# A Perceiver block on one core: self-attention's output projection as three float32r products

## The reference

```
x = x + xattn(layernorm(x), ctx, ctx)      # 16 heads of 16, Wq Wk Wv Wo with biases
x = x + attn(layernorm(x))                 # 16 heads of 16, causal, w_qkv, w_out with biases
x = x + ffn(layernorm(x))                  # ternary weights, rows scaled to 127 levels, SiLU gate, inner 1024

def attn(x):
    q, k, v = split(x @ w_qkv + b_qkv)     # heads of 16
    att = softmax(causal(q k^T / 4))
    return (att v) @ w_out + b_out         # the product that the change is about
```

## Time and profile before

| what | value |
|---|---|
| median of 3 runs | 918.96 us (917.99 to 919.00) |
| profiled execution, its own time | 916.78 us |
| span in it, first to last instruction | 915.0 us |
| PE busy | 876.1 us, 96% of the span |
| DVE busy | 758.4 us, 83% |
| ACT busy | 695.8 us, 76% |
| POOL busy | 431.2 us, 47% |
| mean granted TensorE clock | 0.997 |
| cross-attention, self-attention, feed-forward | about 0 to 550, 550 to 775, 775 to 915 us |

### The profile page before, as it was taken

The page is one execution under the profiler, slowest core; times in us unless marked ns, Lnnn a source line. Parts: engine busy times, 40 slices in busy tenths (PEclk is TensorE's granted clock), DMA queues, the critical chain, the costliest instruction groups (busy, mean ns, idle before and its releaser), DMA issues.

```text
span 915.0 us, 28319 instructions
## 1 busy us (share of the span) xinstructions
PE 876.1 (96%) x9666; PEld 732.9 (80%) x9666; DVE 758.4 (83%) x1587; ACT 695.8 (76%) x2046; POOL 431.2 (47%) x643
## 2 busy tenths in 40 slices
PE   6999999999999999999999988999999998899997
PEld 5888988888888888888988976887878775566664
DVE  5878878888888888877887777988888887999996
ACT  4787887776777777778777765777777767899996
POOL 3333334233333333333443226666666662777775
PEclk9999999999999999999999999999999999999999
DMA  6222111110111011111111100000000000001001
GB/s 181 96 90 80 41 46 29 42 49 30 40 46 40 29 46 40 36 39 40 46 29 40 34 2 1 3 1 1 1 0 0 1 2 2 24 30 35 29 32 39
DMA packets 31637, 31.86 MB, mean 35 GB/s; under 512 B 3280, under 2 KB 30800, under 8 KB 31568
## 3 DMA queue, kind: packets, MB, share of 16 engines
q1 hardware_dynamic: 30448, 30.47, 10.9%
q10 hardware_dynamic: 1120, 0.59, 0.2%
HBM read 26.86 MB, written 4.19 MB: 34 GB/s over the span
## 4 chain that ended last, share of the span: by engine, by line
PE 76%; ACT 12%; issue 5%; DVE 4%; POOL 2%; DMA 0%; ACTq 0%; POOLq 0%; SPq 0%; DVEq 0%
PE psum L342 11%; PE psum L297 9%; PE psum L329 9%; PE psum L312 9%; PE psum L368 6%; PE psum L665 4%; ACT probs L1017 4%; PE psum L703 3%; PE psum L377 3%; PE psum L714 3%; PE psum L284 3%; ACT probs L503 3%; PE psum L750 2%; PE psum L684 2%; PE psum L350 2%
## 5 line engine op out<-in xcount | busy, mean ns | idle before, releaser
L503 ACT ACTIVATE probs<-psum,nmax 128x256 f32<-128x256 f32 x512 | 237.3, 488 | 63.1 <-DVE nmax L460 62.3
L460 DVE TENSOR_REDUCE nmax<-psum 128x2 f32<-128x512 f32 x256 | 158.9, 682 | 24.3 <-PE psum L329 23.6
L511 POOL TENSOR_TENSOR rstd<-vare,minus_half 128x1 f32<-128x1 f32 x96 | 53.1, 553 | 153.8 <-DVE vare L398 151.3
L342 PE MATMUL psum<-id_sb,probs 128*128 128x128 f32 x1024 | 124.6, 273 | 0.5 <-ACT probs L503 0.5
L527 POOL TENSOR_TENSOR cl<-c_sb,ch 128x512 fp32r<-128x512 f32 x64 | 81.6, 1275 | 78.8 <-ACT ch L478 78.8
L342 PEld LDWEIGHTS psum<-id_sb,probs 128*128 128x128 f32 x1024 | 113.0, 140 | 3.4 <-ACT probs L503 2.8
L484 ACT ACTIVATE probsT<-psum 128x512 f32<-128x512 f32 x160 | 89.3, 603 | 30.7 <-PE psum L342 30.5
L503 ACT ACTIVATION_READ_ACCUMULATOR probs<-psum,nmax 128x1 f32 x512 | 112.6, 220 | 0.0
L534 POOL TENSOR_TENSOR rm<-rinv,hm_sb 128x256 f32<-128x256 f32 x64 | 39.7, 620 | 120.6 <-DVE rinv L437 120.6
L329 PE MATMUL psum<-k_sb,qb 32*128 32x256 f32 x1024 | 88.8, 400 | 3.8 <-DVE k_sb L413 1.8
L329 PEld LDWEIGHTS psum<-k_sb,qb 32*128 32x128 f32 x1024 | 62.2, 184 | 15.3 <-issue 10.8
(11 more groups left out here) (141 smaller groups left out, 2338.9 us busy)
## 6 DMA issues: line engine op xcount, KB each, us to landing
c_sb<-in_ctx_t SPq DMA_DIRECT2D x64, 256.0 KB, 2.7
x_sb<-in_x SPq DMA_DIRECT2D x32, 128.0 KB, 2.4
out<-y_sb SPq DMA_DIRECT2D x32, 128.0 KB, 1.7
w_all<-in_w_gate SPq DMA_DIRECT2D x1, 1024.0 KB, 6.4
w_all<-in_w_up SPq DMA_DIRECT2D x1, 1024.0 KB, 5.1
w_all<-in_w_down SPq DMA_DIRECT2D x1, 1024.0 KB, 6.6
wqkv_sb<-in_w_qkv SPq DMA_DIRECT2D x1, 768.0 KB, 5.7
wk_sb<-in_wk ACTq DMA_DIRECT2D x1, 256.0 KB, 3.8
```

What stands on the lines that cost most here:

```text
L342: last = nc.tensor.transpose(sp[g][:, c:c + P], probs[:, 2 * g + u, kh * P:(kh + 1) * P], id_sb[:])
L460: nc.vector.tensor_reduce(nmax[:, 2 * g:2 * g + 2], sp[g].rearrange("p (u s) -> p u s", u=2), AX.X, ALU.max, negate=True).then_inc(max_don ...
L503: nc.scalar.activation(probs[:, j, :], sp[g][:, u * S:(u + 1) * S], ACT.Exp, bias=nmax[:, j:j + 1], accum_out=rsum[:, j:j + 1]).then_inc(e ...
L511: nc.gpsimd.tensor_tensor(rstd[:], vare[:], minus_half[:], ALU.pow).then_inc(ln.rstd_done, 1)
```

## The change

The high and low parts of w_out (w2oh, w2ol) are made as a fourth step of the split in cross-attention: on ACT in tile 25, on POOL in tile 26, whose written-out tiles go on to 27. In self-attention, ACT makes oh, the float32r copy of oT2, for tile t-1 in body t, behind its copies of v; POOL makes ol = oT2 - oh behind rm (in bodies up to 25) and ahead of kbd4. TensorE then does six float32r matmuls in place of two float32 ones (four records), and waits for ol instead of oT2. Tiles 30 and 31 (`t >= NT - 2`) stay as they are.

```diff
+        w2oh, w2ol = sb("w2oh", [P, KT, D], F32R), sb("w2ol", [P, KT, D], F32R)
+        oh, ol = sb("oh", [P, KT, P], F32R), sb("ol", [P, KT, P], F32R)
...
         def act_w2h(a, i):
             a.wait_ge(w2_in, 16 * len(SET2))
-            nc.scalar.activation(w2h_p[:, i, :], wqkv_p[:, i, :], ACT.Copy).then_inc(w2h_split, 1)
+            if i < 3:
+                nc.scalar.activation(w2h_p[:, i, :], wqkv_p[:, i, :], ACT.Copy).then_inc(w2h_split, 1)
+            else:
+                nc.scalar.activation(w2oh[:], wout_sb[:], ACT.Copy).then_inc(w2h_split, 1)
...
+            else:
+                nc.gpsimd.tensor_tensor(w2ol[:], wout_sb[:], w2oh[:].bitcast(F32),
+                                        ALU.subtract).then_inc(w2l_split, 1)
...
         def pe_out2(pe, t, turned=None):
-            pe.wait_ge(o2_ev, t + 1)
             pe.wait_ge(y2_ev, t)
             pe.wait_ge(xh_done, t + 6 if turned is None else turned)
-            for k in range(KT):
-                last = nc.tensor.matmul(y2_ps, oT2[:, k, :], wout_sb[:, k, :],
-                                        start=k == 0, stop=k == KT - 1)
+            if isinstance(t, int) and t >= NT - 2:
+                pe.wait_ge(o2_ev, t + 1)
+                for k in range(KT):
+                    last = nc.tensor.matmul(y2_ps, oT2[:, k, :], wout_sb[:, k, :],
+                                            start=k == 0, stop=k == KT - 1)
+                last.then_inc(y2_mm, 1)
+                return
+            pe.wait_ge(ol2_done, t + 1)
+            for n, (o, w) in enumerate(((oh, w2oh), (oh, w2ol), (ol, w2oh))):
+                for k in range(KT):
+                    last = nc.tensor.matmul(y2_ps, o[:, k, :], w[:, k, :],
+                                            start=n + k == 0, stop=n == 2 and k == KT - 1)
             last.then_inc(y2_mm, 1)
...
         def dve_o2(v, t):
             v.wait_ge(pv2_mm, t + 1)
             v.wait_ge(r2_ev, t + 1)
-            v.wait_ge(y2_mm, t)
+            if t < NT - 1:
+                v.wait_ge(ol2_done, t)
+            else:
+                v.wait_ge(y2_mm, t)
             nc.vector.tensor_tensor(oT2[:], o2_ps, r2_sb, ALU.mult).then_inc(o2_ev, 1)
...
+        def act_oh2(a, t):
+            a.wait_ge(o2_ev, t + 1)
+            a.wait_ge(y2_mm, t)
+            nc.scalar.activation(oh[:], oT2[:], ACT.Copy).then_inc(oh2_done, 1)
...
+        def pool_ol2(p, t):
+            p.wait_ge(oh2_done, t + 1)
+            nc.gpsimd.tensor_tensor(ol[:], oT2[:], oh[:].bitcast(F32), ALU.subtract)\
+              .then_inc(ol2_done, 1)
...
-                pe.wait_ge(w2l_split, 3)
+                pe.wait_ge(w2l_split, 4)
...
-                    body(22 + i, 11 + i // 2, i % 2, w2=i if i < 3 else None)
+                    body(22 + i, 11 + i // 2, i % 2, w2=i)
...
                     act_v2(a, t, t % 2)
+                    if 0 < t < NT - 1:
+                        act_oh2(a, t - 1)
...
-                for i in range(3):
+                for i in range(4):
                     body(23 + i, (23 + i) // 2, (23 + i) % 2, i)
-                with p.Fori(13, NT // 2 - 1) as n:
+                body(27, 13, 1)
+                with p.Fori(14, NT // 2 - 1) as n:
...
                     if t < NT - 6:
                         pool_rm2(p, t)
+                    if 0 < t < NT - 1:
+                        pool_ol2(p, t - 1)
                     if t + 2 < NT:
```

More of the change, by code:

```diff
@@ L240, in block_kernel @@
         o_ev = sem("o_ev")
+        oh2_done = sem("oh2_done")
+        ol2_done = sem("ol2_done")
         y_mm = sem("y_mm")
@@ L595, in act_w2h @@
             a.wait_ge(w2_in, 16 * len(SET2))
-            nc.scalar.activation(w2h_p[:, i, :], wqkv_p[:, i, :], ACT.Copy).then_inc(w2h_split, 1)
+            if i < 3:
+                nc.scalar.activation(w2h_p[:, i, :], wqkv_p[:, i, :], ACT.Copy).then_inc(w2h_split, 1)
+            else:
+                nc.scalar.activation(w2oh[:], wout_sb[:], ACT.Copy).then_inc(w2h_split, 1)
         def pool_w2l(p, i):
             p.wait_ge(w2h_split, i + 1)
-            nc.gpsimd.tensor_tensor(w2l_p[:, i, :], wqkv_p[:, i, :], w2h_p[:, i, :].bitcast(F32),
-                                    ALU.subtract).then_inc(w2l_split, 1)
+            if i < 3:
+                nc.gpsimd.tensor_tensor(w2l_p[:, i, :], wqkv_p[:, i, :], w2h_p[:, i, :].bitcast(F32),
+                                        ALU.subtract).then_inc(w2l_split, 1)
+            else:
+                nc.gpsimd.tensor_tensor(w2ol[:], wout_sb[:], w2oh[:].bitcast(F32),
+                                        ALU.subtract).then_inc(w2l_split, 1)
         b_set = sem("b_set")
```

## The result

The changed kernel takes 920.98 us (median of 16 runs, 919.83 to 922.43), the kernel before 918.05 us on the same chips (16 runs, 916.83 to 919.92). The ratio is 1.003, 95% interval 1.0022 to 1.0038: **slower by 2.9 us**, where +2.45 was forecast.

The account below looks back on a forecast made before the run. TensorE alone bounds the loop, with GpSimd on the path from body 26. Gain of 3.45 us up to body 25 against 5.9 lost in the last bodies: +2.45, on 918.96 giving 921.4 us; range 918.8 to 924.2.

Parts of the forecast that it names:

- The projection's price: Loop's output projection: six float32r records at 0.71 us against four float32 at 0.86, 0.15 us saved a tile.
- The ring in the last bodies: Bodies 26 to 30: oh, ol, kbd4 and rm follow each y addition, 8.15 us a turn; +5.9 us in all.
- The split of the weights: Cross-attention: one more ACT copy and a 1.29 us GpSimd subtraction, covered by TensorE's own work, so no cost.
- ol's cover in the loop: Loop: ol ends at 654.80, TensorE loads the projection's weights at 655.29; 0.49 us to spare, so ol is hidden.
- VectorE's margin: Loop, before the y addition: 0.07 of VectorE's 0.22 us idle time is left, so it does not take over.
- Only ol's own length: Last bodies: oh is never late, kbd4 moves by 0.73 us in bodies 26, 27, 29; 917.1 us, chance 0.12.
- The gain in the loop is lost: Loop: xl holds up xn tile by tile, the period stays as long; +5.9 alone, 924.9 us, chance 0.13.
- TensorE's clock falls: Bodies 28 and 29: TensorE drops to 1.2 GHz after waits of 2 and 3 us, adding 1.2; 922.6 us, chance 0.25.

Follow-up runs that it names:

- the two kernels that have one half of the tiles each: The changed kernel with float32r only in tiles 25 to 29 (924.39 us, ratio 1.0077), and with tiles 25 to 29 back to float32 (913.92 us, 0.995).
- the subtraction without a wait: The changed kernel with tiles 25 to 29 in float32, plus an unused GpSimd subtraction of ol's size ahead of kbd4 in bodies 26 to 30: 916.58 us.

## Why the prediction was right

- *The projection's price.* 0.15 us a tile by the forecast; 0.86 less 0.70 on the chain, and the period 6.57 to 6.42 us. Bodies 1 to 25: -3.52 us against 3.45. Its parts are a little off and cancel: bodies 4 to 24 gave 3.03 us where 3.15 was taken, bodies 1 to 3 gave 0.49 where 0.3 was.
- *The ring in the last bodies.* +5.9 us forecast, +5.90 us from body 25 to 31; the waits 1.4, 1.3, 2, 3 and 1.4 us forecast, 1.42, 1.50, 1.93, 3.19 and 1.25 found; a turn of 8.15 us forecast, 8.16 and 8.21 found. Counted from body 25, the transposes of bodies 26 to 30 come 0.58, 1.44, 3.37, 5.61 and 6.88 us later than before, where 0.75, 1.45, 3.35, 5.55 and 6.87 were forecast. This is close, and in part by luck: the small terms of each turn were rounded. That the loss is there and nowhere else is shown by the two kernels that have one half of the tiles each. That it takes ol's wait besides its length is shown by the subtraction without a wait.
- *The split of the weights* costs next to nothing: 0.2 us at most by the traces.
- *ol's cover in the loop.* 0.49 us to spare was too small; it is 0.76. The tile of the earlier trace rows was not a typical one: xl began 0.45 us behind the end of its copy there, where in the next tile (copy L800 657.86 to 658.24, xl at 658.38) and in nearly all others of the loop it is 0.14 us, as in the changed kernel's tile above. All of GpSimd's chain up to ol stands that much earlier. This did not touch the sum.
- *VectorE's margin.* "Close, but it holds" was right for the 0.07 us; it holds against a further small instruction too.
- *The rivals.* "Only ol's own length" fell with the 4 us that the wait adds. "The gain in the loop is lost" fell with the period: xn takes 0.33 us in every tile of the changed kernel's loop, so ol never holds it up. "TensorE's clock falls" was not in the profiled execution's last bodies in spite of the wait of 3.19 us, but it is in the three other profiled kernels with these last bodies: at the 1.2 us priced in tiles 25 to 29 alone, at 0.15 and 1.0 us in the two with more work in the loop. It is not a rival that fell but one that holds in some executions.
- *Between forecast and result.* 2.45 against 2.9 us lies within the interval (2.0 to 3.5 us). The profiled pair differs by 3.3 us, of which 1.2 is the clock's fall at 550.8 us that only one of the two had. The forecast had no term for such falls, and they account for an estimated 0.7 of the 2.9 us; without them 2.1 to 2.2 us are left, a little under the 2.45. That the absolute 921.4 us came within 0.4 of 920.98 is luck too: it was built on 918.96, a median of three runs that is 0.9 above that of the sixteen, 918.05, while the difference was forecast 0.5 too small.

## What to carry to other kernels

A cheaper instruction on the bounding engine pays in the tiles where that engine bounds; where a hand-written order changes at the end of a stage, the same step has to be priced again there, behind whatever it now stands. An in-order engine that gets a waiting instruction ahead of urgent ones passes the wait on to all of them: here 0.7 us of work cost up to 2.2 us a tile (8.21 us where 5.97 had been). The remedy was not less work but its place: with rm, ol, kbd4 to the end, change and order together give 6.2 us where the change took 2.9, and some 1.7 of the 6.2 the order gives by itself.

## What the runs showed of the hardware

- TensorE's granted clock stood at its lower level (0.50, so 1.2 instead of 2.4 GHz) in stretches of 3.4 us, once of 7, that began within waits of 1.9 to 3.2 us or just behind them. One that begins between 565 and 569 us, by a wait of 2.1 us, is in all 14 profiled executions. The others come in some and not in others of nearly the same schedule: by the wait of 2.91 us near 550 us it fell in 8 of the 14, in the changed kernel and not in the kernel before; at 767.2 us it fell after 3.19 us in one kernel, and not in another with the same wait.
- The cost of such a fall was not the same each time. At 550.8 us it was 1.56 us, at 767.2 us 1.24. With more for GpSimd in the loop it fell at 758.6 us, in front of the longest wait: that wait is 2.10 us instead of 3.19, and 25 to 31 is only 0.15 us longer (43.22 us). With more for VectorE two falls together cost 1.0 us. Where TensorE would wait for GpSimd anyway, slower matmuls take the place of the wait.
- Twenty-four one-column VectorE instructions more in self-attention made feed-forward 1.4 us longer, by idle times of 0.30 us once in eight tiles, and forty-eight did not. The profile names GpSimd's fgu as what ended the idle time, but without the added instructions L929 starts before that fgu does. That the place of the instructions in the program decides fits with this; what it is in the chip was not tried. A difference of 0.15% between two kernels can come from this alone.
